# A block of FFN, attention and FFN: each expert computed for its own tokens alone, instead of for all tokens with coefficients

## The reference

```python
x = x + 0.5 * ffn(layernorm(x))
x = x + attention(layernorm(x))
x = x + 0.5 * ffn(layernorm(x))

def ffn(x):                       # 1024 x 256, 16 experts of 176, top 4
    shared = (silu(x @ Wg.T) * (x @ Wu.T)) @ Wd.T       # hidden size 704
    shared = shared * sigmoid(x @ sgate_w.T)
    w = softmax(x @ gate_w.T); topk_w, topk_ids = top_k(w, 4)
    for e in range(16):
        coef = sum(where(topk_ids == e, topk_w, 0), axis=-1)
        out += (silu(x @ w1[e].T) * (x @ w3[e].T)) @ w2[e].T * coef[:, None]
    return shared + out
```

## Time and profile before

| | |
|---|---|
| median of 3 runs (lowest to highest) | 797.39 us (797.12 to 801.84) |
| the profiled execution, and its span in the trace | 796.24 us, 794.4 us |
| busy: PE, DVE, ACT, POOL | 735.7, 460.9, 373.9, 189.7 us |
| mean granted clock of PE | 0.967 |
| moved by DMA | 44.37 MB |

### The profile page before, as it was taken

The page is one execution under the profiler, slowest core; times in us unless marked ns, Lnnn a source line. Parts: engine busy times, 40 slices in busy tenths (PEclk is TensorE's granted clock), DMA queues, the critical chain, the costliest instruction groups (busy, mean ns, idle before and its releaser), DMA issues.

```text
span 794.4 us, 13291 instructions
## 1 busy us (share of the span) xinstructions
PE 735.7 (93%) x4776; PEld 391.3 (49%) x4776; DVE 460.9 (58%) x942; ACT 373.9 (47%) x569; POOL 189.7 (24%) x158
## 2 busy tenths in 40 slices
PE   4699999999996677999999999997879999999997
PEld 2356666656564233333333434543446656556665
DVE  6555454545548977899988877643533333333334
ACT  6434343333334466746657667776622222222222
POOL 1273333333344412000000000000143333333332
PEclk9999999999998689999999999999699999999999
DMA  5353333334310000000000000000042222221212
GB/s 170 101 148 112 119 119 113 113 120 133 116 54 1 0 1 1 1 1 1 1 2 1 1 1 2 1 1 1 2 112 77 67 65 72 60 79 53 79 53 80
DMA packets 16169, 44.37 MB, mean 56 GB/s; under 512 B 2658, under 2 KB 5090, under 8 KB 16132
## 3 DMA queue, kind: packets, MB, share of 16 engines
q1 hardware_dynamic: 12388, 33.65, 14.4%
q10 hardware_dynamic: 3744, 10.23, 3.9%
HBM read 42.68 MB, written 1.19 MB: 55 GB/s over the span
## 4 chain that ended last, share of the span: by engine, by line
PE 82%; DVE 6%; issue 4%; ACT 4%; DMA 2%; POOL 1%; SPq 1%; DVEq 0%; ACTq 0%; POOLq 0%
PE psum L857 53%; PE psum L1021 8%; PE psum L1005 8%; PE psum L994 7%; PE psum L992 2%; PE psum L1008 2%; DVE m_part L807 2%; PE psum L979 1%; ACT kT L563 1%; PE psum L1028 1%; DMA coef_dram<-oT 1%; POOL R L379 1%; DVE kaug L797 1%; DMA R<-coef_dram 1%; DMA x_res<-x_dram 1%
## 5 line engine op out<-in xcount | busy, mean ns | idle before, releaser
L857 PE MATMUL psum<-xT,W_hi 128*128 128x512 f16 x880 | 265.2, 383 | 0.0
L379 POOL TENSOR_TENSOR R<-R 128x512 f32<-128x512 f32 x112 | 152.5, 1363 | 298.0 <-DVE R L718 250.1
L807 DVE TENSOR_REDUCE m_part<-psum 128x1 f32<-128x512 f32 (+3 forms) x384 | 188.1, 550 | 42.3 <-PE psum L994 40.1
L704 DVE SCALAR_TENSOR_TENSOR R<-psum,R 128x512 f32<-128x512 f32 x108 | 74.7, 691 | 226.0 <-ACT R L491 225.9
L491 ACT ACTIVATE R<-psum 128x512 f32<-128x512 f32 x108 | 64.4, 597 | 265.5 <-PE psum L857 265.5
L857 PE MATMUL psum<-W_hi,R 128*128 (+1 forms) x896 | 166.5, 275 | 11.5 <-DVE R L718 11.5
L578 ACT ACTIVATE R<-psum 128x1024 f32<-128x1024 f32 x144 | 141.8, 1024 | 68.1 <-PE psum L1005 45.6
L857 PE MATMUL psum<-xT,W_lo 128*128 128x512 f16 x440 | 168.2, 382 | 0.0
L857 PEld LDWEIGHTS psum<-xT,W_hi 128*128 (+1 forms) x880 | 86.8, 99 | 83.4 <-issue 3.5
L857 PE MATMUL psum<-W_lo,R 128*128 (+1 forms) x448 | 123.3, 275 | 0.0
L994 PE MATMUL psum<-kT,qT 128*128 128x512 f16 (+3 forms) x384 | 105.8, 334 | 1.0 <-DVE m_part L807 0.6
(11 more groups left out here) (101 smaller groups left out, 457.3 us busy)
## 6 DMA issues: line engine op xcount, KB each, us to landing
R<-coef_dram SPq DMA_DIRECT2D x64, 256.0 KB, 3.8
w_stage<-w_dram ACTq DMA_DIRECT2D x26, 384.0 KB, 2.9
R<-coef_dram SPq DMA_DIRECT2D x8, 448.0 KB, 3.5
R<-coef_dram SPq DMA_DIRECT2D x8, 384.0 KB, 3.4
R<-coef_dram SPq DMA_DIRECT2D x8, 320.0 KB, 3.5
R<-coef_dram SPq DMA_DIRECT2D x8, 192.0 KB, 3.7
x_res<-x_dram SPq DMA_DIRECT2D x8, 128.0 KB, 2.2
R<-coef_dram SPq DMA_DIRECT2D x8, 128.0 KB, 3.1
```

Source lines behind the costliest of these rows:

```text
L379: nc.gpsimd.tensor_tensor(hc[:, c, :], v[:, j, c, :], C[:, j, c * CH:(c + 1) * CH], ALU.mult).then_inc(s_hc[c], 1)
L704: nc.vector.scalar_tensor_tensor(out=v[:, j, c, :], in0=bank[2 + c][:, :], scalar=1.0 / WS, in1=sg[:, c, :], op0=ALU.mult, op1=ALU.mult).t ...
L807: nc.vector.tensor_reduce(m_part[:, h, kc:kc + 1], ps[:, 0:n], axis=AX.X, op=ALU.max).then_inc(free_of(e), 1)
L857: ins = nc.tensor.matmul(o, stat(a, k), mov(b, k), start=first and n == 0, stop=last and n == 3 * k_parts - 1, **kw)
```

## The change

Per FFN, in order:

1. The shared part is computed as before, but alone: `NS` = 6 steps instead of 28, with `down` one step behind `gate_up`, and its output is multiplied by the sigmoid when DVE adds it to `x_res` (`shared_out`).
2. DVE marks the chosen experts (`sel`), PE multiplies the marks by a matrix with ones above the diagonal and by matrices of ones (9 matmuls), which gives for each token and expert its rank among that expert's tokens. DVE makes from it the row of each of a token's four copies (`slots`), and tables by tile: expert, first row, row of padding (`tables`).
3. POOL issues 32 indirect DMAs (8 token tiles by 4 choices), each of which writes 128 token rows of 1 KB (high and low part) to their rows in `xg_dram` (`scatter`). SP fills 128 rows behind each expert's last token (`fill_pads`, 16 register loads and DMAs).
4. `NX` = 47 tiles of 128 rows are computed, however the tokens fall: SP loads a tile's rows from DRAM at a register's address, PE transposes them, reads the number of the tile's expert from SBUF into a register, multiplies by that expert's weights at a register address, and ACT, DVE and PE make the hidden part, transpose it and multiply by `w2`. SP stores each result of 128 x 256 f32 to `y_dram`. No product by a coefficient and no POOL work is in this loop.
5. When all results are stored, POOL issues 32 indirect DMAs which gather for each token tile and choice 128 rows of 1 KB into one of 8 buffers, and DVE multiplies each by its coefficient and adds it to `x_res` (`combine`).

The weights of the experts have a layout of their own (`W_ex`), and in the first FFN all weights go through a staging ring of four in 27 jobs (`staging_jobs`), all of which lie in the six shared steps: SP loads, ACT and DVE make the high and the low part, some of them in several pieces. The second store of the output is by token tile. The attention is the same but for its tiles being made later by POOL (`attention_tiles`), and for waits.

```diff
+NS = MT - MX
+NX = T * 4 // P + NE - 1
+FB = FE - P
+WGU = 2 * KC * FE
+WE_N = 2 * WGU + 4 * D
+OFF_A, OFF_B = 2 * WGU, 2 * WGU + 2 * D
+NST = 4
+CAP = T + P
+NG_E = 4
 WC = 3 * D
 NG = NE + 1
 NC = 2
@@ -38,24 +47,6 @@
 UH = NH // GHI
 AHEAD = 1
...
+def staging_jobs():
+    jobs = [("S", s) for s in range(NS)]
+    for g, pairs in enumerate(((0, 2, 4), (6, 8, 10), (12, 14, 16), (18, 20))):
+        jobs += [("P", m) for m in pairs] + [("A", g), ("B", g)]
+    return jobs + [("Q", k) for k in range(KC)]
...
+        def loads_up_to(j):
+            return sum(2 if jobs[i][0] == "B" else 1 for i in range(j % NST, j + 1, NST))
...
+        def jobs_of_position(s, c):
+            counts = (1, 1, 2, 2, 2, 2, 2, 2, 3, 3, 3, 3)
+            first = 1 + sum(counts[:2 * s + c])
+            return range(first, first + counts[2 * s + c])
...
+            def load_tokens(f, s):
+                n = f * NX + s
+                if s == 0:
+                    sp.wait_ge(s_pad, 16 * NE * (f + 1))
+                    sp.wait_ge(s_scat, 16 * NK * (f + 1))
+                if n >= 8:
+                    sp.wait_ge(s_xgp, n - 7)
+                r = sp.value_load(tab_r[0:1, s:s + 1], min_val=0, max_val=NE * CAP - P)
+                sp.dma_start(xg[:, n % 8, :], xg_dram[bass.ds(r, P), :]).then_inc(s_xg[n % 8], 16)
+            def fill_pads(f):
+                sp.wait_ge(s_tab, f + 1)
+                for e in range(NE):
+                    r = sp.value_load(tab_p[0:1, e:e + 1], min_val=0, max_val=NE * CAP - P)
+                    sp.dma_start(xg_dram[bass.ds(r, P), :],
+                                 x_hl[:, 0].rearrange("p a d -> p (a d)")).then_inc(s_pad, 16)
+            def store_result(f, s):
+                n = f * NX + s
+                sp.wait_ge(s_ysb[n % 2], n // 2 + 1)
+                sp.dma_start(y_dram[f][s * P:(s + 1) * P, :], y_sb[:, n % 4, :]).then_inc(s_yst[n % 4], 16)
+            def experts(f):
+                for s in range(4):
+                    load_tokens(f, s)
+                for s in range(NX):
+                    if s + 4 < NX:
+                        load_tokens(f, s + 4)
+                    store_result(f, s)
...
+            def attention_tiles():
+                pool.wait_ge(s_wlo, len(jobs))
                 nc.gpsimd.memset(kT[:, :, :].rearrange("p g n -> p (g n)").bitcast(F32), 0.0)
                 nc.gpsimd.memset(kaug[:], 0.0)
                 nc.gpsimd.memset(vals[:], 0.0).then_inc(s_pool, 1)
-                pool.wait_ge(s_pool, 1)
+                pool.wait_ge(s_pool, 2)
                 nc.gpsimd.memset(kaug[:, :, :, 24:26], 1.0)
                 nc.gpsimd.memset(vals[:, :, :, HD:HD + 1], 1.0).then_inc(s_ready, 1)
...
+            def scatter(f):
+                pool.wait_ge(s_slot, f + 1)
+                pool.wait_ge(s_xl[0], (2 * f + 1) * TPC)
+                pool.wait_ge(s_xl[1], (2 * f + 1) * TPC)
+                for t in range(TT):
+                    for k in range(TOPK):
+                        nc.gpsimd.indirect_dma_start(
+                            xg_dram, bass.IndirectOffsetOnAxis(ap=slot[:, t, k:k + 1], axis=0),
+                            x_hl[:, t].rearrange("p a d -> p (a d)"), None).then_inc(s_scat, 16)
+            def gather(f):
+                pool.wait_ge(s_y_row, f + 1)
+                for i in range(4):
+                    last = max(n for n in range((f + 1) * NX) if n % 4 == i)
+                    pool.wait_ge(s_yst[i], 16 * (last // 4 + 1))
+                for j in range(NK):
+                    if j >= 8:
+                        pool.wait_ge(s_comb, f * NK + j - 7)
+                    nc.gpsimd.indirect_dma_start(
+                        y_got[:, j % 8, :], None, y_dram[f],
+                        bass.IndirectOffsetOnAxis(ap=y_row[:, j // TOPK, j % TOPK:j % TOPK + 1], axis=0)
+                    ).then_inc(s_got[j % 8], 16)
+            constants()
             low_parts(0)
-            ffn(0, constants)
+            scatter(0)
+            attention_tiles()
+            gather(0)
+            nc.gpsimd.memset(qaug[:, :, :, 24:32], 0.0).then_inc(s_ready, 1)
             low_parts(1)
-
...
+                for s in range(-1, NX + 2):
+                    n = f * NX + s
+                    if s + 1 < NX:
+                        tokens_out(n + 1)
+                    if 0 <= s < NX:
+                        silu_expert(n)
+                    if s >= 2 and n % 2:
+                        result_out(n - 2)
+                    if 0 <= s < NX:
+                        high_expert(n)
...
+                nc.vector.tensor_scalar(sel[:, 0:TT, :], rest[:, :, 0:NE], 0.0, None, ALU.is_lt).then_inc(s_sel, 1)
...
+            def slots(f):
+                dve.wait_ge(s_rank, f + 1)
+                ins = nc.vector.tensor_copy(rank, bank[7][:, 0:(TT + 1) * NE])
+                ins.then_inc(s_rank_read, 1)
+                dve.wait_ge(s_rank_read, f + 1)
+                if f == 0:
+                    dve.wait_ge(s_iota, 1)
+                chosen(key, e_row[:])
+                for t in range(TT):
+                    ins = nc.vector.max(key8[:, t, :], key[:, t, :])
+                link(ins)
+                nc.vector.tensor_scalar(slot[:], key8[:, :, 0:TOPK], -1.0, None, ALU.add).then_inc(s_slot, 1)
...
+            def combine(f, tiles):
+                for t in tiles:
+                    for k in range(TOPK):
+                        j = t * TOPK + k
+                        uses = sum(1 for i in range(f * NK + j + 1) if i % 8 == j % 8)
+                        dve.wait_ge(s_got[j % 8], 16 * uses)
+                        if k:
+                            dve.wait_ge(s_comb, f * NK + j)
+                        else:
+                            dve.wait_ge(s_shared, f * TT + t + 1)
+                        nc.vector.scalar_tensor_tensor(out=x_res[:, t, :], in0=y_got[:, j % 8, :],
+                                                       scalar=ck[:, t, k:k + 1], in1=x_res[:, t, :], op0=ALU.mult,
+                                                       op1=ALU.add).then_inc(s_comb, 1)
...
+                for s in range(NS):
                     for c in range(NC):
+                        gated(f, s, c)
+                        if f == 0:
+                            for j in jobs_of_position(s, c):
+                                weights_low(j)
+                        low(f, s, c)
+                    if s == 0:
+                        slots(f)
+                    if s == 1:
+                        tables(f)
+                        if f == 0:
+                            dve.wait_ge(s_late, N_LATE)
+                            nc.vector.tensor_copy(identb[:], ident[:])
+                            nc.vector.tensor_copy(maskb[:], maskf)
+                for t in range(TT):
+                    shared_out(f, t)
+                link(nc.vector.memset(h_hl[:, :, :, FE:192], 0.0))
+                for s in range(NX + 2):
+                    n = f * NX + s
+                    if s < NX:
+                        gated_expert(n)
+                    if 1 <= s < NX + 1:
+                        hidden_out(n - 1)
+                    if s >= 2 and n % 2 == 0:
+                        result_out(n - 2)
+                    if s < NX:
+                        low_expert(n)
...
+            def tokens(n):
+                pe.wait_ge(s_xg[n % 8], 16 * (n // 8 + 1))
+                if n >= 2:
+                    pe.wait_ge(s_xgT, n - 1)
+                ps = x_bank[n % 2][:, 0:256].bitcast(F16)
+                for q in range(2 * KC):
+                    ins = nc.tensor.transpose(ps[:, q * P:(q + 1) * P], xg[:, n % 8, q * P:(q + 1) * P], ident16[:])
+                ins.then_inc(s_xgp, 1)
+            def expert_gate_up(f, s, e):
+                n = f * NX + s
+                if f == 0 and s < NE and s % NG_E == 0:
+                    pe.wait_ge(s_wlo, group_jobs[s // NG_E])
+                pe.wait_ge(s_xgT, n + 1)
+                if n >= 2:
+                    pe.wait_ge(s_he, n - 1)
+                ins = split_product(
+                    gu_bank[n % 2][:, 0:2 * FE],
+                    lambda a, k: xgT[:, n % 2, (a * KC + k) * P:(a * KC + k + 1) * P],
+                    lambda b, k: W_ex[:, bass.ds(e, 1), b * WGU + k * 2 * FE:b * WGU + (k + 1) * 2 * FE]
+                    .rearrange("p o n -> p (o n)"), KC)
+                ins.then_inc(s_gue, 1)
...
+                pe.wait_ge(s_tab, f + 1)
+                expert = {}
+                for s in range(-1, NX + 2):
+                    n = f * NX + s
+                    if s + 1 < NX:
+                        tokens(n + 1)
+                    if 0 <= s < NX:
+                        expert[s] = pe.value_load(tab_e[0:1, s:s + 1], min_val=0, max_val=NE - 1)
+                        expert_gate_up(f, s, expert[s])
+                    if s >= 2:
+                        if s == 2:
+                            pe.wait_ge(s_shared, (f + 1) * TT)
```

(70 more changed lines are left out.)

558 lines of the change are left out of this document (328 added, 230 removed).

## The result

The changed kernel takes 932.45 us (926.77 to 935.53) where the kernel before, on the same chip, takes 797.75: 1.167 times as long, 95% interval 1.160 to 1.174. The prediction said slower, but by 26 us and not by 135, and its range ended at 900. The profiled execution took 935.53 us.

What follows compares the result with a forecast made beforehand. PE, busy for 93% of the span, was taken to bound the kernel. The old span of 794.4 us plus 22.7 (first FFN) and 4 (second) made 821.1, with 1.84 around it 823 us; range 765 to 900.

Steps and rivals of the forecast that it cites:

- the tile's period: Expert loop: PE is the longest engine and sets 2.5 us a tile, 47 tiles 117.5 us in each FFN.
- rival B: Expert tiles: the register load stops PE, a tile takes 3.0 to 3.6 us, total 870 to 926; chance 0.18.
- the tile's period is above 3: Expert loop: a sign named in advance that would prove the prediction wrong; the forecast took 2.5 us.
- PE's own 2.2 us a tile: Expert tile on PE: transposes 0.8, six matmuls of 352 columns 0.88, five of 256 columns 0.53 us.
- POOL's price: Scatter and gather: one indirect DMA costs POOL 1.3 us, so 32 of them take 41.6 us.
- Rival A: Gathers and second scatter: POOL issues cheaply, kernel faster from 1.02 us per indirect DMA down; 769 at 0.6; chance 0.23.
- Rival C: Scatters and gathers: DVE and POOL lock each other out, adding 61 us, total 884; chance 0.14.
- 64 gathers pay 0.42 each: Gathers of both FFNs: descriptors wait for DVE's additions, 27 us in all, if DVE and POOL lock each other out.
- The first start: First FFN: experts begin at 99.5 us, behind pads that follow the last weight load, near 80.
- DVE's weights: First FFN's shared part: DVE needs 71 us where PE needs 47, sets the pace, and the part ends near 87.
- The second start: Second FFN: experts begin 59.5 us from its start, after 12.5 to the slots, scatter 41.6, landing and first tile 5.4.
- the gain of 172 us of PE in each FFN: Both FFNs: 22 of 28 steps go, taking 172 us of PE work from each.

Runs made afterwards that it cites:

- static7: Over look7, each tile's expert number is a program constant (s // 3), so PE loads no register; 794.39 us (0.997).
- look5: The changed kernel with tokens loaded 5 tiles ahead instead of 4; 809.09 us (1.014).
- look7: The changed kernel with tokens loaded 7 tiles ahead instead of 4; 796.76 us (0.999).
- onein7: Over look7, DVE makes the weights' low parts with one SBUF input instead of two, as zeros; 791.43 us in one execution.
- single7: Over look7, the first FFN's pads issued one by one behind weight loads from job 11 on; 798.41 us (1.001), at another time 783.26 (0.983).
- repeat4: The changed kernel itself, measured again at another time; 917.55 us (1.149).

## Why the prediction was wrong

**The failed step** is the tile's period: "no chain but ACT's own [...] lies within a tile, and PE is the longest", and from it 2.5 us. The prediction costed each engine (2.2, 1.5, 1.45) and looked for a chain inside a tile. It never costed the tokens' way: 94 loads and 94 stores are in the diff, in one queue, each load behind a store that waits for a result. The distance of 4 was taken as cover without a word; it covers two tiles, 4.5 us, and the round takes 7 with the 2.05 us landing in it. Measured 3.5 us a tile, 53 and 45 us too much in the two FFNs, which is 98 of the 113 us between the forecast's span and the profiled one. The terms were in reach: landings of 2.2 and 2.3, an issue of 0.43. The prediction named "the tile's period is above 3" as what would refute it, and rival B's price of 3.0 to 3.6 us contains the measured one, but its cause was the register load, and static7 shows that this costs 0.03. The price was covered by luck, the mechanism wasn't covered at all.

**PE's own 2.2 us a tile** was right: 2.27 once nothing stands in the way. The clock is part of the loop's price, not a cause of its own. With gaps in each round the clock granted was 0.86 and 0.91, and the six gate and up matmuls took 1.94 us in one round and 1.06 in the next; with PE busy for 67.86 and 70.00 of 70 us in look5 and look7 it was 1.00.

**POOL's price.** Predicted 1.3 us, measured 0.95 of work and 0.30 to the next, 1.25: 32 gathers took 39.9 us to the last one's end, and the last landed 2.71 us behind its start. Rival A, 1.02 or less, is out. The Trainium skill's 2.0 us of fixed time for a software-issued DMA (DMA: Bandwidth & Descriptors, Anatomy of one DMA) isn't what each costs in a row: these rows put 1.25 there, and 2.71 on the last one's landing, which agrees with the Trainium skill where it puts most of the fixed time on completion.

**Rival C** is half right, as onein7 shows: the first scatter grows by 9 to 11 us beside DVE's low parts. "64 gathers pay 0.42 each" is wrong: L556 took 942, 949 and 1042 ns (min, median, max), with DVE adding pairs of SBUF inputs beside it. The Trainium skill's "DVE blocks DMA" trap (SBUF — State Buffer) is told of DVE's instructions in a 2-port perf mode. Here single scatters grew beside instructions with two SBUF inputs and lengths up to 1.22 us, and the gathers beside the 0.49 us additions did not; which of DVE's instructions run in such a mode, no trace here shows.

**The first start** came at 103.2 and not 99.5. That the pads follow the last load and cost 14 was right in kind (17.1 measured). Loads of the weights, "hidden" in the prediction by a landing of 2.9 us, took 5 and stood on the chain three times (`kT` is the buffer that the weights are staged in):

```profile
48.19 4.99 DMA kT<-w_dram
...
61.31 4.83 DMA kT<-w_dram
...
72.16 5.14 DMA kT<-w_dram
```

DVE's weights were predicted to set the pace of the shared part; they and these landings did, in turn, and it ended at 89.5 us (87 predicted). The first start was set by the pads, which the prediction also names as a sign of being wrong, though its own sum has the pads end behind the shared part: single7, which moves them, has its first tile at 91.5.

**The second start** was predicted at 59.5 us and came at 74.3. The scatter began 11.2 us behind the first gate_up (12.5 predicted) and took 41.6 (41.6 predicted). The other 15 are the slow stretch, of which the trace of before, without an indirect DMA, has no sign; in the same kernel's other run (repeat4) the first tile comes 46.6 us behind the first scatter (predicted 47.0), in this one 63.1.

**Where the gain of 172 us of PE in each FFN went**, then, in the profiled execution: 181 and 173 us of expert tiles, of which 107 are PE's own work (47 x 2.27); 42 and 44 us of gather; starts of 103 and 74 us. Without the loop (look7) the sum is 796.76, and even then the change only breaks even, as 40 us of gather in each FFN, and 42 of scatter in the second, stand on the path where PE had been full before.

## What to carry to other kernels

Count a prefetch in time, not in buffers: where loads and stores share a queue in program order, follow one round (result, store's issue, load's issue, landing, first use, next result) and divide it by the tiles that are under way in it. If that is above the busiest engine's time for a tile, one more buffer ahead is worth more than any engine's work: a 4 that became a 7 gave 136 us here, or 121 if both are taken without the slow stretch. And when work moves from a full engine to gathers and scatters in series, price the ends first, where nothing can stand beside them.

## What the runs showed of the hardware

- One indirect DMA of 128 rows cost POOL 0.95 us and 0.30 to the next, whether it wrote rows of 1 KB (scatter) or read them (gather); single scatters took up to 3.37 us beside DVE's low parts of the weights.
- A register load from SBUF took SP 0.27 us and PE 0.30, and 0.15 + 0.02 us of register work behind it; on PE it hid.
- Beside an indirect scatter SP went in steps of 0.70 us for 31 us and PE in multiples of 0.70 us for the last 18 of them, in one run of a kernel (the changed kernel; single7 alike) and not in another run of the same: 15 us of the total, seen in 4 of 18 profiles with a scatter, three of them taken one after another on one chip, and explained by none.
